# A context unit's second piece loaded in two parts by features, in a Perceiver layer on one core

## The reference, cut to what matters

```python
x = x + xattn(layernorm(x), ctx)        # x: [8, 64, 2048], ctx: [8, 1601, 2048], float32
x = x + attn(layernorm(x), w_q, w_k, w_v, w_o)
x = x + ffn(layernorm(x), A_w, B_w, Wq_w, keys)

def xattn(query, key):                  # the part that the change touches
    e = softmax(einsum('bqd,bkd->bqk', query, key))
    return einsum('bqk,bkd->bqd', e, key)
```

## Time and profile before

| what | value |
|---|---|
| timed runs, median (lowest to highest) | 1555.49 us (1553.21 to 1561.1) |
| profiled execution, whole | 1550.1 us |
| its span, from first to last instruction | 1548.3 us |
| TensorE, mean granted clock over the span | 0.988 |
| cross attention, up to TensorE's last products with values | about 490 us |

### The profile page before, as it was taken

How to read it: one execution, slowest core, us unless ns; L and a number is a source line. 1 busy time by engine, 2 the same in 40 slices (tenths; PEclk the granted TensorE clock), 3 DMA queues, 4 the chain that set the end, 5 groups by cost and what they waited for, 6 DMA issues and landing times.

```text
span 1548.3 us, 23956 instructions
## 1 busy us (share of the span) xinstructions
PE 1460.9 (94%) x9593; PEld 1035.5 (67%) x9593; DVE 775.5 (50%) x1055; ACT 497.6 (32%) x656; POOL 601.3 (39%) x310
## 2 busy tenths in 40 slices
PE   3889899889996999999999999999999999999999
PEld 1333333333333888888888888888888888878777
DVE  4566656657655203554465455446437430367333
ACT  1143443443433323333323333234224232232321
POOL 0041242242152233663663654664656644420000
PEclk9999999999997999999999999999999999999999
DMA  9858878788744242232332332332331352220113
GB/s 356 296 173 255 309 226 258 281 239 258 269 135 154 95 124 77 87 109 81 108 96 66 108 108 70 100 101 81 108 107 56 109 163 85 93 95 1 44 67 135
DMA packets 178637, 219.93 MB, mean 142 GB/s; under 512 B 5904, under 2 KB 104208, under 8 KB 175920
## 3 DMA queue, kind: packets, MB, share of 16 engines
q1 hardware_dynamic: 150912, 166.42, 34.2%
q10 hardware_dynamic: 27648, 52.44, 10.0%
HBM read 207.82 MB, written 10.49 MB: 141 GB/s over the span
## 4 chain that ended last, share of the span: by engine, by line
PE 82%; DVE 5%; DMA 4%; ACT 2%; issue 2%; SPq 2%; POOL 1%; ACTq 0%; DVEq 0%; POOLq 0%
PE ps L807 15%; PE ps L809 15%; PE ps L808 15%; PE ps L743 10%; PE ps L1847 5%; PE ps L1849 5%; PE ps L1848 5%; PE ps L695 4%; DMA xa_raw<-in_ctx 3%; PE ps L715 2%; DVE xa_kt L594 2%; PE ps L1787 2%; SPq L320 1%; PE ps L1940 1%; DVE xa_kt L598 1%
## 5 line engine op out<-in xcount | busy, mean ns | idle before, releaser
L807 PE MATMUL ps<-h_hi,w_hi 128*128 128x512 f32 x800 | 315.5, 394 | 1.2 <-DVE h_lo L1503 1.1
L1235 POOL TENSOR_TENSOR w_lo<-raw,w_hi 128x2048 fp32r<-128x2048 f32 (+1 forms) x52 | 212.8, 4096 | 258.9 <-ACT w_hi L1300 216.6
L809 PE MATMUL ps<-h_hi,w_lo 128*128 128x512 f32 x800 | 311.8, 390 | 0.0
L808 PE MATMUL ps<-h_lo,w_hi 128*128 128x512 f32 x800 | 311.4, 389 | 0.0
L594 DVE STREAM_TRANSPOSE xa_kt<-xa_raw 128x832 f32<-128x832 f32 (+1 forms) x208 | 192.9, 993 | 125.6 <-PE ps L695 112.7
L695 PE MATMUL ps<-xa_kt,xa_q_t 128*64 128x416 f32 (+2 forms) x1024 | 197.8, 522 | 23.0 <-DVE xa_kt L594 11.2
L551 POOL TENSOR_TENSOR xa_x<-xa_x,xa_tmp 64x512 f32<-64x512 f32 x88 | 110.9, 1285 | 270.8 <-ACT xa_tmp L434 266.8
L743 PE MATMUL ps<-xa_raw,xa_e_t 32*64 32x512 f32 (+1 forms) x3264 | 182.6, 589 | 0.0
L807 PEld LDWEIGHTS ps<-h_hi,w_hi 128*128 128x128 f32 x800 | 150.2, 188 | 36.4 <-issue 6.5
L1591 DVE TENSOR_TENSOR rows<-rows,ps 128x512 f32<-128x512 f32 x168 | 115.6, 688 | 116.0 <-PE ps L1849 116.0
L809 PEld LDWEIGHTS ps<-h_hi,w_lo 128*128 128x128 f32 x800 | 150.1, 188 | 31.8
(11 more groups left out here) (231 smaller groups left out, 1894.5 us busy)
## 6 DMA issues: line engine op xcount, KB each, us to landing
raw<-in_L_attn_w_q SPq DMA_DIRECT2D x32, 1024.0 KB, 5.9
raw<-in_L_attn_w_o SPq DMA_DIRECT2D x30, 1024.0 KB, 5.0
xa_raw<-in_ctx SPq DMA_DIRECT2D x48, 384.0 KB, 7.0
xa_raw<-in_ctx ACTq DMA_DIRECT2D x16, 832.0 KB
xa_raw<-in_ctx SPq DMA_DIRECT2D x16, 832.0 KB
xa_raw<-in_ctx ACTq DMA_DIRECT2D x32, 384.0 KB, 8.0
xa_raw<-in_ctx SPq DMA_DIRECT2D x16, 768.0 KB
xa_raw<-in_ctx ACTq DMA_DIRECT2D x16, 768.0 KB
```

The costliest lines, as they stand in the source:

```text
L807: pe.matmul(out, hi, mov_hi, start=first, stop=False)
L808: pe.matmul(out, hi, mov_lo, start=False, stop=False)
L809: return pe.matmul(out, lo, mov_hi, start=False, stop=last)
L1235: pool.tensor_tensor(w_lo[:, n % 2, part], raw[:, n % 2, part], w_hi[:, n % 2, part].bitcast(F32), ALU.subtract).then_inc(w_lo_done, 1)
```

## The change

The second piece of every odd unit (the first units of the start among them) is loaded in two parts by features: columns 0 to 255 of each quadrant, then columns 256 to 511. Each run is 1 KB then, not 2 KB, and each part has as many issues as the whole piece had. Both parts are issued at the place where the piece was. Each place gets a third semaphore, for the second part. VectorE waits ahead of chunk 0 for the first part, and ahead of chunk 8, the first that reads column 256 or a later one, for the second.

```diff
+FEATURE_PARTS = 2
...
+def second_loads(u):
+
+    n = sum(len(piece_runs(v, NPIECE - 1, i)) for v in range(u % PLACES, u + 1, PLACES) if v % SIDES for i in range(QUADRANTS))
+    return 16 * n
...
+def feature_parts(u, g):
+
+    return FEATURE_PARTS if u % SIDES and g == NPIECE - 1 else 1
...
-    raw_in = [[sem(f"xa_raw_in{p}{g}") for g in range(NPIECE)] for p in range(PLACES)]
+    raw_in = [[sem(f"xa_raw_in{p}{g}") for g in range(NPIECE + FEATURE_PARTS - 1)] for p in range(PLACES)]
...
         at = UNIT * place(u)
-        for i in QUEUE_QUADS[queue]:
+        parts = feature_parts(u, g)
+        for p, i in [(p, i) for p in range(parts) for i in QUEUE_QUADS[queue]]:
+            n0, n1 = p * 512 // parts, (p + 1) * 512 // parts
             for j0, j1 in piece_runs(u, g, i):
                 k0 = KEY0[x] + a * COLS[x] + SQ * j0
-                src = ctx[b, k0:k0 + SQ * (j1 - j0), i * 512:(i + 1) * 512].rearrange("(k c) n -> c k n", c=SQ)
-                eng.dma_start(raw[quadrant(i), at + j0:at + j1, :], src).then_inc(raw_in[place(u)][g], 16)
+                src = ctx[b, k0:k0 + SQ * (j1 - j0), i * 512 + n0:i * 512 + n1].rearrange("(k c) n -> c k n", c=SQ)
+                eng.dma_start(raw[quadrant(i), at + j0:at + j1, n0:n1], src).then_inc(raw_in[place(u)][g + p], 16)
...
                     for g in range(NPIECE):
                         dve.wait_ge(raw_in[place(u)][g], piece_loads(u, g))
+            if c == DC // FEATURE_PARTS:
+                dve.wait_ge(raw_in[place(us[1])][NPIECE], second_loads(us[1]))
```

More of the change, by code:

```diff
@@ L46 @@
 NPIECE = len(PIECES) - 1
+FEATURE_PARTS = 2
+PART = 512 // FEATURE_PARTS
 EVENTS = NPIECE + 1
```

## The result

The changed kernel takes 1560.26 us (median of 20 runs, 1555.44 to 1565.36) against 1553.86 us of the kernel before (20 runs beside them): a ratio of 1.0043, 95% interval 1.0031 to 1.0054. It is slower by 6.4 us, where 1.0 us was forecast; the time lies inside the range.

The account below looks back on a forecast made before the run. TensorE led the chain (82%), with context loads causing few waits; -2.7 us of waits removed and +3.65 us of ScalarE issues gave about +1.0 us, 1556.5 us on the timed runs' scale; range 1549.5 to 1562.5 us.

Parts of the forecast that it names:

- The start: Stage 1's first K^T chunk, at 44.71 us before, comes earlier as its first part lands sooner: -1.5 us.
- Stages 6 and 10: K^T's load waits of 0.32 and 0.88 us at these stages go whole: -1.2 us.
- stage 11: K^T's load wait of 4.12 us shrinks to 1 to 2 us, at most 0.5 us gained; counted as nothing.
- The wait at chunk 8: VectorE's added wait for the second part, landing 2.6 us after the first, is covered by 6 us: no cost.
- Stages 2 and 6: ScalarE's four extra issues in stages 1 and 5 delay the exponentials TensorE waits for: 1.85 + 1.8 = +3.65 us.
- Stages 3, 7, 11 and 13: The 1.85 us delay of ScalarE's issues just fits some 2.1 us idle before the exponentials: no cost, 0.2 us left.
- rival B: ScalarE's issues in odd stages cost over 0.52 us each and it ends slower, 1560.8 to 1571.3 us; chance 0.09.
- The clock: The prediction had no term for TensorE's clock falling behind its gaps at stages 2, 6 and 10.
- Stage 10: Once stage 11's load wait shrinks, the load of the rows of x is late next; no gain taken.
- Rival C: A 1 KB packet takes as long as a 2 KB one: +8.3 us, 1563.8 us, slower; chance 0.04.
- Rival A: Timed runs hold more load waits than the profiled one, so the change gains more: 1551.1 us; chance 0.09.

Follow-up runs that it names:

- experiment 1: The kernel before with ScalarE's four issues of the second piece cut into eight by blocks, runs still 2 KB: 1562.42 us, ratio 1.0043.
- experiment 3: The changed kernel with 38 idle transposes on TensorE ahead of its wait for the exponentials in stages 2, 6 and 10: 1553.58 us, ratio 0.9997.
- experiment 4: The kernel before with 26, 22 and 75 idle transposes on TensorE ahead of the probabilities of stages 2, 6 and 15: 1551.92 us, ratio 0.9982.
- experiment 7: The kernel before with only the start's units 1 and 3 split: 1550.1 us, ratio 0.9983; with idle transposes too: 1547.18 us, ratio 0.9953.
- experiment 5: The changed kernel, ScalarE's second-part issues in odd stages moved behind the four scaled copies: 1555.72 us, ratio 1.0014; with idle transposes too: 1546.39 us.

## Why the prediction was right, and where its sum was not

The time is in the range, and the sign and the main mechanism are as forecast: the waits for loads that the change removes were worth little, and ScalarE's four extra issues are paid at stages 2 and 6. But the sum was +1.0 us and the measurement +6.4. That the range held it is partly luck: on the prediction's scale the result is 1555.49 + 6.4 = 1561.9 us, 0.6 us inside the upper end, and that end was drawn for dearer issues and for scatter, not for what filled it. By its steps:

- *The start, -1.5 us.* Right as far as shown: the median gains 2.6 us (0.2 to 5.1) where the start alone is split. The row that was to show it (first chunk near 43.2 us) was at 44.70 in the changed kernel and at 42.19 to 44.42 in the seven others of the table; one trace was not enough to see 1.5 us there.
- *Stages 6 and 10, -1.2 us, and stage 11, nothing.* Right, -1.4 and -0.5 us. Stage 11's wait did not shrink to 1 to 2 us but went.
- *The wait at chunk 8: nothing.* Right in all traces with the split on both queues, even with ScalarE's part issued 5 us later. (The second part was to land 2.2 + 0.2 = 2.4 us behind the first, not 2.6; nothing hangs on it.)
- *Stages 2 and 6, +3.65 us.* Right: 1.69 + 1.84 = 3.5 us; experiment 1 shows at stage 2 that the issues do it alone.
- *Stages 3, 7, 11 and 13 "just fit".* Wrong, and by a mechanism that neither the sum nor rival B had. B looked for the dearer issue in the depth of the queue and set its point at 0.52 us each. The issues were at 0.45 us in general, but in stages 3, 7 and 11 one of the eight took 1.63, 1.53 and 1.37 us beside a packet of instructions. A cover with 0.2 us to spare was counted as whole; it was worth +3.0 us. In experiment 1's trace such issues stood in all three blocks again (1.61, 1.57 and 1.54 us), in experiment 3's in none, and there nothing was uncovered: this term is partly chance, and its share of the median is not known.
- *The clock: no term at all.* With the step before, this failed most: +4.1 us behind the three gaps in the trace, net of the next item about +2.6. The prediction took a gap's growth at its length. But a stretch of TensorE's work behind such a gap also ran in part at 1.2 GHz: 3.73 us of gap had 1.36 us more behind it, 5.42 us had 1.37 + 0.98. The row was there: 3.03 us for probabilities which take 1.67 in most stages.
- *Stage 10.* In the kernel before TensorE's wait stood ahead of stage 11's scores, so that the 16 score products behind it took the slow clock (5.29 us; 3.63 in experiment 4). With the load gone, the wait was for the exponentials, and probabilities and products pay. The prediction asked what is late next and named the rows of x; it was ScalarE's block, delayed by the issues.

Rival C is out (377 GB/s at 1 KB). Rival A, that timed runs hold more load waits, has this for it: the rate of the start's loads did differ between executions, by 8%, and in the traces of kernels with whole refills (before, 4 and both of 7) K^T waited for loads behind the start at two to five stages. But the changed kernel, whose trace has none of these waits after the start, was slower all the same.

## What to carry to other kernels

Cost a wait of TensorE at its length and at what the clock takes behind it: look whether the first stretch after each gap runs as fast as the same stretch elsewhere, before adding to the gap. Where a DMA has to be issued on a busy engine, put each issue into a wait that the engine has anyway (here 0.3 us between copies that are paced by another engine), not as a block in front of work that others wait for; a cover that fits within tenths of a microsecond is none. And compare a start that is bound by loads over several traces, each against its rate, before saying that it did not move.

## What the runs showed of the hardware that was not expected

- *A packet of instructions beside DMA issues.* Over the thirteen traces, between 80 and 460 us, ScalarE has 1686 DMA issues, and 57 of them took over 1.2 us. Of these 57, 54 overlapped a 16 KB packet of the instruction queue (0.9 to 1.7 us long), as 148 shorter ones did; of the 1484 issues that overlapped none, 3 were so long. Of SP's 84 issues over 1.2 us, 68 overlapped one. A longer block of issues has more chances to meet a packet. That the packet is the cause was not tried apart.
- *Queues with unequal packets.* With 1 KB packets on SP's queue and 2 KB on ScalarE's, what SP's queue carries fell behind by about 3 us at the start, against a whole start at the same rate, while the two queues moved equal numbers of packets (2077 and 2070); with 1 KB on both, nothing fell behind.
- *Idle transposes pay.* 26 transposes of the identity (3.06 us) in a wait of TensorE returned 1.4 us at stage 2 of the kernel before, and 38 returned 1.4 + 1.0 us at stage 2 of the changed one, with what TensorE waited for left as it was. Behind 38 at stage 10 TensorE stood 1.89 us more, and the rows there stayed slow.
- *Gaps of one length, different slow stretches.* Ahead of stage 2, 4.22 us in experiment 5 and 4.23 us in experiment 7 (the runs without transposes):

```profile
108.12 2.35 PE L733 MATMUL ps<-ident,xa_expo 128*128 128x128 f32 x13 [4.22 <-ACT xa_expo L412]
110.41 12.31 PE L761 MATMUL ps<-xa_raw,xa_e_t 32*64 32x512 f32 x208
```

```profile
107.00 3.03 PE L732 MATMUL ps<-ident,xa_expo 128*128 128x128 f32 x13 [4.23 <-ACT xa_expo L412]
109.96 12.91 PE L760 MATMUL ps<-xa_raw,xa_e_t 32*64 32x512 f32 x208
```

Against 1.67 and 11.41 us at full clock, the first pair paid 1.6 us and the second 2.9, more than the 2.4 us behind the changed kernel's 5.42. So the price of one gap is read from a trace, not from its length.
